# A two-layer token tower on one core: softmax heads as 64-row tiles side by side, q and k stored once, expert weights split in the first stage, rows of the second norm by ScalarE, gate bias by a matmul

## The reference

```python
h = take(W.T, x) + b + pe
# block 1: 8 heads of 16, causal, scores normalised by their row's causal mean and variance, no softmax
t = dots - mu;  attn = t * rsqrt(s + EPS) * norm_g + norm_b;  h = h + (attn @ v) @ w_out + b_out
# block 2: a layer norm of a layer norm, 2 heads of 64, softmax, then 8 gated experts
q, k = l2norm(q) * sqrt(64) * qn_g, l2norm(k) * sqrt(64) * kn_g
o = softmax(causal(q @ k.T / 8)) @ v;  y = o @ Wo
gate = softmax(y @ gate_W + gate_b);  hid = gelu(y @ W1[e] + b1[e])
h = h + sum_e gate[e] * (hid @ W2[e] + b2[e])
```

## Time and profile before

| | us |
|---|---|
| runs of the kernel | 930.7, 931.53, 932.92, median 931.53 |
| the profiled execution, own time | 936.06 |
| its span | 934.3 |
| mean granted TensorE clock | 0.943 |

### The profile page before, as it was taken

How to read it: one execution, slowest core, us unless ns; L and a number is a source line. 1 busy time by engine, 2 the same in 40 slices (tenths; PEclk the granted TensorE clock), 3 DMA queues, 4 the chain that set the end, 5 groups by cost and what they waited for, 6 DMA issues and landing times.

```text
span 934.3 us, 20793 instructions
## 1 busy us (share of the span) xinstructions
PE 816.1 (87%) x7860; PEld 588.3 (63%) x7860; DVE 724.7 (78%) x1719; ACT 516.0 (55%) x1071; POOL 339.7 (36%) x380
## 2 busy tenths in 40 slices
PE   1796999999966577798889888999999999999997
PEld 1574777777734335565555556667777777777775
DVE  5644677666589985667667764799999999999997
ACT  1332444344356655777898898665555555555553
POOL 7465665555454433656676676100000000000000
PEclk9877999999878866999999999999999999999999
DMA  4110000000000000000000000000000000000000
GB/s 125 28 35 18 1 0 0 0 0 0 1 0 1 0 1 1 25 24 24 24 25 25 24 2 2 1 2 13 2 13 5 11 13 2 13 2 13 1 13 13
DMA packets 9477, 11.68 MB, mean 13 GB/s; under 512 B 1832, under 2 KB 6704, under 8 KB 9264
## 3 DMA queue, kind: packets, MB, share of 16 engines
q1 hardware_dynamic: 8368, 8.43, 3.1%
q0 software_dynamic: 1024, 2.10, 0.8%
HBM read 8.43 MB, written 2.10 MB: 11 GB/s over the span
## 4 chain that ended last, share of the span: by engine, by line
PE 62%; DVE 16%; ACT 8%; POOL 7%; issue 7%; DMA 0%; DVEq 0%; ACTq 0%; POOLq 0%
PE ps L929 60%; POOL plo L343 3%; ACT phi L519 2%; ACT p L518 2%; DVE y L674 2%; POOL h_all L222 2%; DVE qkn L741 2%; DVE khl L751 1%; DVE ql L749 1%; DVE ss L726 1%; DVE mx L806 1%; PE ps L1088 1%; ACT arena L393 1%; DVE x L720 1%; ACT ql L487 1%
## 5 line engine op out<-in xcount | busy, mean ns | idle before, releaser
L537 ACT ACTIVATE cst<-ps,col 128x512 f32<-128x512 f32 x256 | 176.0, 689 | 160.1 <-PE ps L929 159.3
L929 PE MATMUL ps<-y,arena 128*128 128x512 f16 (+1 forms) x896 | 247.3, 426 | 17.6 <-DVE y L674 16.3
L929 PEld LDWEIGHTS ps<-arena,sq 128*128 128x128 f16 x3072 | 192.1, 98 | 62.1 <-DVE sq L913 4.6
L929 PE MATMUL ps<-arena,sq 128*128 128x128 f16 x3072 | 213.0, 219 | 0.6 <-DVE sq L913 0.5
L913 DVE TENSOR_TENSOR sq<-cst,sq 128x512 f16<-128x512 f32 x256 | 175.8, 687 | 4.4
L343 POOL TENSOR_TENSOR plo<-p,phi 128x512 f16<-128x512 f32 (+2 forms) x120 | 125.1, 1061 | 72.9 <-ACT phi L519 69.5
L908 DVE CAST sq<-cst 128x512 f16<-128x512 f32 x256 | 108.8, 425 | 9.3 <-ACT cst L537 1.8
L929 PEld LDWEIGHTS ps<-y,arena 128*128 128x128 f16 (+1 forms) x896 | 75.7, 113 | 56.7 <-issue 20.9
L806 DVE TENSOR_REDUCE mx<-ps 128x1 f32<-128x512 f32 (+3 forms) x160 | 90.6, 603 | 13.6 <-PE ps L929 12.7
L518 ACT ACTIVATE p<-ps 128x512 f32<-128x512 f32 (+3 forms) x160 | 89.5, 560 | 19.9 <-PE ps L929 19.1
L519 ACT ACTIVATE phi<-ps 128x512 f16<-128x512 f32 (+3 forms) x160 | 90.0, 563 | 0.0
(11 more groups left out here) (151 smaller groups left out, 1264.3 us busy)
## 6 DMA issues: line engine op xcount, KB each, us to landing
sq<-w_rows SPq DMA_DIRECT2D x16, 256.0 KB, 2.7
out<-h_all SPq DMA_DIRECT2D x32, 64.0 KB, 1.6
cst<-consts SPq DMA_DIRECT2D x1, 1294.0 KB, 5.8
h_all<-emb_rows,idx POOLq DMA_INDIRECT x32, 2.5
wqkv<-w_qkv SPq DMA_DIRECT2D x1, 192.0 KB, 5.7
wsm<-w_sm SPq DMA_DIRECT2D x1, 192.0 KB
row<-rows SPq DMA_DIRECT2D x1, 140.0 KB, 2.4
c<-consts SPq DMA_DIRECT2D x1, 96.0 KB
```

Of the source, the lines that this page charges most:

```text
L537: a.activation(hid[:, f], ps[:, HBANK[f], :], ACT.Gelu_apprx_tanh, bias=col[:, K_B1 + k:K_B1 + k + 1], scale=1.0 / WS).then_inc(S["hid_rea ...
L929: return t_.matmul(o, l, r, start=start, stop=stop, skip_group_check=True)
```

## The change

Nothing changes in what is computed, except that row maxima are taken of the product of the high halves alone. The parts:

- **Storage.** `kh`, `kl`, `qh`, `ql` are [128, 4096] f16, head 0 in rows 0 to 63, head 1 in 64 to 127, each stored once. `arena` holds only weights; the causal stage's tiles and later the softmax stage's share a new `room`. The doubled forms, the memset of ones and the doubled copy in `unit_qk` go; `unit_qk` is one operation per chunk, PE transposes four blocks, ACT writes two high halves, DVE two low halves, all of 128 rows and 256 columns.
- **Scores.** A step is now both heads of a pair (80 steps, 8 items). Each product is a 64-row matmul per head, heads alternating, into banks in turn of three; the row maximum enters by a product of a one-hot tile with `qm`. Masks are 64-row products too, two per head. The scores of step s wait for the exponentials of the first head of step s-1.
- **Maxima.** One part is a pair of 64-row matmuls into banks 3 and 4 and one reduction over both; the next part waits for it. DVE writes the maximum itself, and the transposing matmul is with minus the identity. The parts' places come from a planner that spreads them by due step.
- **Weights.** `weights_high` and `weights_low` move to the ends of the causal steps 1 to 13; piece n goes to step n*13//16+1, so steps 1, 5 and 9 have two. DVE's and ACT's first use of the tiles shared with them waits for all 16.
- **Loops.** The four `Fori` loops are written out.
- **Second norm.** From chunk 2 on POOL makes -mean*factor with two more small operations and ACT scales the rows (`scaled_rows`).
- **Gate.** The bias comes in by a one-row matmul on PE; DVE has five small operations in place of seven; ACT's copy of the transposed gate has the scale. Output parts come after every item of both heads, in slots 1, 2, 3, 6, 7 (PE), 1, 2, 4, 6 (ACT), 3, 5, 8 (DVE).
- **Low halves** by POOL three of four, in the last 18 steps one of two.
- **Entry to the experts** waits for all heads' outputs; banks there are 0 to 3 up, 4 and 6 down, 5 for the last output part.

```diff
-        khl = sb("khl", [P, HS, B * N], F16)
-        kh1 = sb("kh1", [DS + 1, HS, B * N], F16)
-        qhh = sb("qhh", [P, HS, B * N], F16)
-        ql = sb("ql", [DS + 1, HS, B * N], F16)
+        kh = sb("kh", [P, B * N], F16)
+        kl = sb("kl", [P, B * N], F16)
+        qh = sb("qh", [P, B * N], F16)
+        ql = sb("ql", [P, B * N], F16)
...
+        WAT = {c: [n for n in range(NPIECE) if n * 13 // NPIECE + 1 == c] for c in range(NT)}
...
                 if more:
                     out_bias(c + 1)
+                for n in WAT[c]:
+                    weights_low(n)
             step_a(1, 0, tail=False)
             gather(24, T)
-            with pool.Fori(2, NT - 3, 2) as c:
+            for c in range(2, NT - 2, 2):
...
                 sums_out(c, cur, 1, read=read)
+                for n in WAT[c]:
+                    weights_high(n)
...
+            def scaled_rows(c):
+                par = c % 2
+                act.wait_ge(S["rr_ready"], c + 1)
+                for b in range(B):
+                    last = a.activation(x2[par][:, b], h_all[:, 2 * c + b, :], ACT.Identity,
+                                        bias=rr[par][:, 3, b:b + 1], scale=rr[par][:, 1, b:b + 1])
+                last.then_inc(S["x2_ready"], 1)
...
             def high_qk(c):
+                act.wait_ge(S["qkd_ps"], c + 1)
+                bank = t_bank(c)
+                a.activation(chunk(qh, c), ps[:, bank, 0:2 * P].rearrange("p (b t) -> p b t", b=B),
+                             ACT.Copy, scale=qkg8[:])
+                a.activation(chunk(kh, c), ps[:, bank, 2 * P:].rearrange("p (b t) -> p b t", b=B),
+                             ACT.Copy, scale=col[:, K_KG:K_KG + 1]).then_inc(S["hi_ready"], 1)
...
+            def pair_scores(it, r, kb, w, k):
...
+                if guard:
+                    pe.wait_ge(*guard)
+                for h in range(HS):
+                    half = slice(h * DS, (h + 1) * DS)
+                    last = mm(ps[:, 3 + h, 0:w], qh[half, q:q + P], kh[half, at:at + w], stop=kb < c)
...
+                last.then_inc(S["sm_ps"], 1)
+                guard = S["sm_used"], k + 1
...
             def scores(s):
...
+                if s:
+                    pe.wait_ge(S["p_ready"], 2 * s - 1)
+                for still, moving in ((kh, qh), (kl, qh), (kh, ql)):
+                    for h in range(HS):
+                        half = slice(h * DS, (h + 1) * DS)
+                        mm(ps[:, (2 * s + h) % 3, lo:], still[half, at:at + P], moving[half, q0 + lo:q0 + CH],
+                           start=still is kh and moving is qh, stop=False)
...
+                if s in FIRST:
+                    pe.wait_ge(S["mrow_sb"], it + 1)
+                for h in range(HS):
+                    half = slice(h * DS, (h + 1) * DS)
+                    last = mm(ps[:, (2 * s + h) % 3, lo:], onehot[half], qm[half, it % 2, lo:], start=False)
...
+            for s in range(NSTEP + LAG + 6):
+                if s < NSTEP:
+                    scores(s)
+                if s < 2:
+                    unit_T(NT - 2 + s)
+                for part in MSLOT.get(s, ()):
+                    pair_scores(*part)
+                if LAG <= s < NSTEP + LAG:
+                    values(s - LAG)
+                if s in RAT:
+                    max_row(RAT[s])
...
-            pe.wait_ge(S["o_used"], len(ITEMS) - 1)
+            pe.wait_ge(S["o_used"], len(ITEMS))
```

More of the change, by code:

```diff
@@ L695, in _ @@
             dve.wait_ge(S["gathered"], 16 * (T - 8))
-            with dve.Fori(2, NT - 3, 2) as c:
+            for c in range(2, NT - 2, 2):
                 for u in range(2):
@@ L1046, in _ @@
             step_a(1, 0, first=True)
-            with pe.Fori(2, NT - 3, 2) as c:
+            for c in range(2, NT - 2, 2):
                 for u in range(2):
@@ L1307, in plan @@
 def plan():
[L1310 to L1318 removed]
+    items = [(c, b) for c in range(NQ) for b in range(B)]
+    steps, first, parts = [], [], []
@@ L1319, in plan @@
+    k = 8
+    for it, (c, b) in enumerate(items):
         first.append(len(steps))
         steps += [(it, 4 * c + d, d, True) for d in range(4)] + [(it, kt, 0, False) for kt in range(4 * c)]
[L1321 to L1326 removed]
@@ L1327, in plan @@
-    o_at = [e - 1 + LAG for e in ends]
-    y_at = [o_at[it] for it in range(1, len(items), 2)]
-    return items, steps, first, mparts, mslot, o_at, y_at
-BTAIL = NT - 2
-PR, QR = 5, 4
-LAG = 3
-YGAP = 3
-ITEMS, STEPS, FIRST, MPARTS, MSLOT, OAT, YAT = plan()
+        if it:
+            for kb in range(c + 1):
+                for r in range(4):
+                    parts.append((it, r, kb, CH if kb < c else (r + 1) * P, k))
+                    k += 1
+    due = [None, 2] + [f - 3 for f in first[2:]]
@@ new lines, in plan @@
+    mslot, done, credit = {}, 0, 0.0
+    for s in range(1, len(steps)):
+        left = [(sum(p[0] <= it for p in parts) - done) / (due[it] - s + 1) for it in range(1, len(items)) if due[it] >= s]
+        credit = min(credit + max(left, default=0), 3.0)
+        while credit > 1 - 1e-6 and done < len(parts):
+            mslot.setdefault(s, []).append(parts[done])
+            done, credit = done + 1, credit - 1
+    assert done == len(parts)
+    for it in range(1, len(items)):
+        assert max(s for s, ps in mslot.items() for p in ps if p[0] == it) <= due[it]
@@ L1337 @@
+    rat = {(3 if it == 1 else first[it] - 2): it for it in range(1, len(items))}
+    o_at = [e - 1 + LAG for e in first[1:] + [len(steps)]]
+    y_at = []
+    for m in range(len(items)):
+        y_at.append(max(o_at[m], y_at[-1] + 8) if m else o_at[0])
+    return items, steps, first, mslot, rat, o_at, y_at
+BTAIL = NT - 2
+PR, QR = 6, 6
+LAG = 2
+K16 = 8
+PE_Y, ACT_Y, DVE_Y = [1, 2, 3, 6, 7], [1, 2, 4, 6], [3, 5, 8]
+ITEMS, STEPS, FIRST, MSLOT, RAT, OAT, YAT = plan()
 NSTEP = len(STEPS)
-NMAX = sum(len(p) for p in MPARTS)
+NMAX = 8 + sum(len(p) for p in MSLOT.values())
```

587 lines of the change are left out of this document (283 added, 304 removed).

## The result

The changed kernel takes 946.42 us (median of 4 runs, 944.23 to 951.2); the kernel before took 932.22 in the same session (930.7 to 934.91). The ratio is 1.0154, 95% interval 1.0129 to 1.0179: slower by 1.5%, where 896 us was forecast. The profiled execution took 947.07 us, its span is 945.2.

What follows compares the result with a forecast made beforehand. Limits by stage: TensorE in causal attention and experts, VectorE in the second norm, none in softmax. Terms +7.0-1.3-18.3-17-6+0.7 sum to -35: 936.06 to 901 us profiled, 896 as median; range 881 to 911.

Steps and rivals of the forecast that it cites:

- Gathers behind the first weights, +7.0: Early causal steps: the last eight gathers start at 73.3 instead of 66.36, behind two weight subtractions on GpSimd; +7.0 us.
- Later pieces hold GpSimd's factors back ...: nothing, and up to 2 us in all: Causal steps: factors 0.8 to 2 us later, hidden under VectorE's wait for TensorE; cost nothing, up to 2 us without cover.
- the loops' 1.3: Causal steps: written-out loops take 12.49 us a step instead of 12.61, over 11 steps; -1.3 us.
- Norm stage, -18.3: Second norm: copy distances fall from 6.02 to 4.6 us for 12 periods, -17.0, and -1.3 for the first two.
- At the 1.2 GHz level ... push the loop to about 4.8: Second norm: at TensorE's low clock, eight 384-wide passes and five transposes lengthen the loop to about 4.8 us.
- First eight double steps, -6: Start of the softmax stage: twelve maximum parts, 28.5 us in place of 34.7; -6 us.
- 72 double steps, -17: Softmax stage from the third item: 121 full, 31 narrower, 21 output parts, 11 paired maximum parts; 184 against 201.5 us.
- Entry to the experts, +0.7: Start of the experts: TensorE waits for the last head's division, +1.1, two fewer small VectorE operations, -0.4; +0.7 us.
- A: Rival, softmax stage: ScalarE governs, 72 steps take 151 us, -50 in place of -17; total 863 us; chance 0.17.
- B: Rival, softmax stage: 144 array mode changes wait out results, 0.16 us more each, +19, nothing won there; 915 us; chance 0.19.
- D: Rival, softmax stage: f16 pairs do not run at once, +67 us, so slower at 963 us; chance 0.04.
- C: Rival, norm stage: TensorE's low clock and order hold the period near 5.4, 10 us less won, plus B's stage; 921; chance 0.06.

Runs made afterwards that it cites:

- runs 4: Changed kernel with GpSimd's weight subtraction behind the next step's coefficients from causal step 2 on, the first two pieces still ahead of the gathers: 936.85 us, ratio 1.0029.
- run 2: Changed kernel with GpSimd's weight subtraction moved from a causal step's end to behind the next step's coefficients: 929.3 us, ratio 0.9968.
- run 12: Kernel before with only the four loops over the causal steps written out: 930.47 us, ratio 0.9977.
- run 10: Changed kernel with the last operation of the variances as a tensor_reduce instead of a tensor_scalar: 935.79 us, ratio 1.0029; once more for its profile, 940.78 us.
- run 1: Changed kernel with the last operation of the variances as a scalar_tensor_tensor, epsilon from a tile, instead of a tensor_scalar: 947.87 us, ratio 1.0145.
- run 6: Changed kernel with the first item's row scores and their reductions placed later in norm steps 9 to 12, where no copy waits: 937.72 us, ratio 1.0054.
- run 9: Changed kernel with the 16 weight pieces split in the softmax stage, behind every fourth double step from the tenth, none in causal steps: 936.59 us, ratio 1.0006.
- f3_five: Changed kernel with the edits of f1_three, three added products in norm steps 1 to 7, and ScalarE's transposed-row copy ahead of the high halves: 904.86 us, ratio 0.9712.
- f1_three: Changed kernel with the edits of run 2, run 5 and run 6 together: 909.75 us, ratio 0.9756.
- run 5: Changed kernel with a double step's second and third row maximum parts behind the products with v and the low halves: 940.14 us, ratio 1.0099.
- run 3: Changed kernel with the 16 weight pieces on causal steps 2 to 13 instead of 1 to 13: 943.29 us, ratio 1.0125.

## Why the prediction was wrong

The parts do what the prediction said they do; some 50 us were lost, nearly all in four places that it priced at nothing or too low: the causal steps (9.3 us worse than forecast), the norm stage (12.2), the first eight double steps (8.4) and the 72 after them (19.2).

- **Gathers behind the first weights, +7.0.** Right: 7.0 in the trace, 7.6 between runs 4 and 2. One hold of 0.84 us stands in that stretch too, and the written-out loops give about as much back (run 12). VectorE's wait is 15.0 us, as announced.
- **"Later pieces hold GpSimd's factors back ...: nothing, and up to 2 us in all".** This step failed. It looked at GpSimd's queue, and priced the subtraction by who waits for GpSimd. Nobody does; it is VectorE's tensor_scalar that is held until the subtraction ends, for 0.84 us in each of 11 steps, 9.2. Less the loops' 1.3 this is the +8.0 of the table; runs 4 and 10 win 9.6 and 10.6. The trace of before had a sign of it that was not read: L644, 256 columns from two SBUF tiles, takes 982 ns beside GpSimd's second state addition and 418 where GpSimd does nothing (249.63). The rule of the Trainium skill given in run 10 spoke against the change.
- **Norm stage, -18.3.** The period was right, 4.46 us against "4.35 us from copy to copy", but only at the full clock. "At the 1.2 GHz level ... push the loop to about 4.8" was mis-sized: with the clock between 0.50 and 0.78 the five periods of run 1's profile have 5.7 in the mean, and two that are at 0.50 throughout (runs 6 and 9) took 6.0. There the loop is another one: ScalarE's queue from the squares to the copy of the transposed rows (3.0 us, with the two added row scalings), then the projection, 2.92 at that level (at 312.55). Why the changed kernel gets less clock in this stage (0.67 from first copy to first exponential, 0.77 before) stays open: at full clock TensorE's busy share of a period is no lower than before, 2.43 of 4.46 us against 2.99 of 5.79. The row scores inside steps 9 to 12 were not priced at all: they cost up to 7.6 us of distances (30.3 for the four, 22.7 in run 6, at a better clock). With the clock held and the row scores moved f3_five has 67.8 us from the first copy to the fifteenth, 16.5 less than the 84.3 of before; f1_three, without the filler, has 67.5.
- **First eight double steps, -6.** Became +2.4. Five of them hold two or three parts in shared banks. The price of 1.24+0.5 a part left out what stands in line behind each; double step 2 took 5.8 us (clock 0.58) and step 3, with three parts, 8.3 (clock 0.50). The order is only part of it: run 5 takes 2.3 us off these eight, and the other 6 of the term no run won back.
- **72 double steps, -17.** Became +2.2. Plain steps were right to 0.02 us (20 of 2.22). Above a base of 150.5 us for all 72 (54 by 2.22, 18 by 1.7), the steps with two parts take 22.4 us more where the term said 11, those with output parts 24.8 where it said 21, and the three transfers of row maxima on other steps 3, which had no term. The wait of 1.32 us was priced ("8x1.4"); the low clock behind it was not. Run 5 brings these steps to the 11 of the forecast, and the 72 steps of f3_five take 192.6 us. Some of the term is luck: in run 2's profile, with the same program there, the 72 take 198.9.
- **Entry to the experts, +0.7.** 1.3: the last values end at 595.9, and the division for both heads (595.90 to 596.83) and a hop stand ahead of the first product at 597.26.
- **Rivals.** A is out: ScalarE waits 0.15 us for TensorE in every plain step. B is out as a mechanism: the values start 0.31 after the last pair, 0.22 of which is the pair's spacing, so a change costs about 0.1 of TensorE's time, and the loop over the exponentials covers it. D is out: the f16 pairs run side by side. C had the right place in the norm stage: its 10 us less stand against 12.2, though its period of 5.4 was not that of the low level, and it had a chance of 0.06. Its total is wrong as a sum: with B's stage (915) and 10 more it is 925, not 921. B has 19 us for waits at the changes of mode, the paragraph before the sum some 10; at 0.1 us a change the runs bear out neither. The one case on the slow side had the wrong mechanism, and 0.05 was left for this side because each unknown was bounded by itself: the work moved beside VectorE had no bound at all.

## What to carry to other kernels

Before moving work onto GpSimd, list what VectorE does at that moment, and in which form it reads SBUF; if something there is on the path, move the one, or give the other a form that stays out of it (one instruction changed here, 10 us). When an engine that held the others up is relieved, price the next loop at both levels of TensorE's clock: as long as VectorE held the period at 5.79 us the clock did not matter, and behind it 4.46 or 6.0 hung on it. An engine's queue is in order: two pieces that share a bank need other work between them, on both engines.

## What the hardware showed unexpectedly

- A 16-column tensor_scalar of VectorE took 1.02 us beside GpSimd's subtraction, and 0.17 without; a tensor_reduce in its place took 0.19. It shows in the chain as "issue", with no releaser.
- Three added products per step, 0.22 us each, kept TensorE at its 2.4 GHz level (granted clock 1.00 over five periods, 0.85 without) and took 3.8 to 6.5 us off that stage; the medians differ by 8.1.
- The same instructions fall into different clocks from one execution to the next: a norm period is 4.46 us in one profile and 6.0 in another, and the softmax stage takes 233.3 or 238.1 us. Runs of one kernel spread by 3 us (run 3) to 15 (run 9), those of the kernel before by 6.
